# Seven block products in two more token groups of the shared experts, with the weight sums made in consecutive items

## The reference, cut to what matters

```python
for e in range(N_SHARED):                       # 2 shared experts
    h = silu(x_flat @ s_w1[e].T) * (x_flat @ s_w3[e].T)
    shared_out = shared_out + h @ s_w2[e].T
...
s = sigmoid(router_in @ W_router.T);  sel = s + router_bias   # top 2 of 8, gates from s
for e in range(N_EXPERTS):
    h = gelu(x_flat @ r_w1[e].T)
    routed_out = routed_out + h @ r_w2[e].T * gates_full[:, e:e + 1]
out = (shared_out / 2 + routed_out) / 4
```

## Time and profile before

| what | us |
|---|---|
| median of three runs | 1938.53 |
| the profiled execution, first to last instruction | 1936.9 |
| TensorE busy | 1899.1 (98%) |
| VectorE busy | 1166.6 (60%) |
| ScalarE busy | 898.0 (46%) |
| DMA engines, mean busy share | 48.3% on the SyncE queues' hardware queue, 10.0% on GpSimd's |

### The profile page before, as it was taken

One profiled execution on the slowest core, in us unless ns is written; L12 is line 12 of the kernel. 1 busy time (PEld: TensorE's weight loads), 2 busy tenths in 40 slices (PEclk: granted clock), 3 DMA queues, 4 the chain that ended last, 5 costly groups with the idle time before them and its releaser, 6 DMA issues. The chain is left out here.

```text
span 1936.9 us, 47260 instructions
## 1 busy us (share of the span) xinstructions
PE 1899.1 (98%) x18896; PEld 1230.9 (64%) x18896; DVE 1166.6 (60%) x2564; ACT 898.0 (46%) x1900; POOL 155.9 (8%) x160
## 2 busy tenths in 40 slices
PE   8999989999999999999999999999999999999997
PEld 7999954444444434444444444457777777899996
DVE  6666646554788656312111116778778886688887
ACT  4444445434112444434333335534334443588886
POOL 0000000000000000211111102111111120000000
PEclk8999999999999999999999999999999999999999
DMA  7033347866353565899999957655454566142233
GB/s 307 14 130 130 132 150 196 236 201 201 129 174 136 174 210 165 194 238 219 216 219 206 199 135 235 195 178 162 138 160 135 159 153 240 57 165 47 47 56 48
DMA packets 305823, 314.02 MB, mean 162 GB/s; under 512 B 228887, under 2 KB 246429, under 8 KB 298718
## 3 DMA queue, kind: packets, MB, share of 16 engines
q1 hardware_dynamic: 292526, 267.53, 48.3%
q0 software_dynamic: 13104, 43.79, 10.0%
HBM read 191.98 MB, written 73.66 MB: 137 GB/s over the span
## 5 line engine op out<-in xcount | busy, mean ns | idle before, releaser
L1275 PE MATMUL sh_p<-xh,arena 128*128 128x512 f16 x1280 | 382.1, 380 | 6.2 <-ACT sh_gated L1550 4.7
L1346 PE MATMUL p<-sh_h_hi,arena 128*128 128x512 f16 x1024 | 304.6, 379 | 1.0 <-DVE sh_h_lo L1925 1.0
L1275 PE MATMUL sh_p<-xl,arena 128*128 128x512 f16 x640 | 243.2, 380 | 0.0
L2286 DVE SCALAR_TENSOR_TENSOR ro_hs<-ro_h,fac,ro_hs 128x512 f16<-128x512 f32 x71 | 53.4, 751 | 297.2 <-ACT ro_hs L2272 297.2
L1275 PEld LDWEIGHTS sh_p<-xh,arena 128*128 128x128 f16 x1280 | 125.2, 98 | 158.8 <-ACT sh_gated L1550 5.2
L2229 PE MATMUL ro_py<-arena,ro_ht 128*128 x852 | 195.0, 379 | 1.8 <-DMA ro_ht<-ro_hs 1.8
L1346 PE MATMUL p<-sh_h_lo,arena 128*128 128x512 f16 x512 | 194.0, 379 | 0.0
L1521 ACT CAST sh_h_hi<-sh_gated 128x512 f16<-128x512 f32 x128 | 79.1, 618 | 231.8 <-DVE sh_gated L2018 205.5
L1346 PEld LDWEIGHTS p<-sh_h_hi,arena 128*128 128x128 f16 x1024 | 96.6, 98 | 107.1 <-DVE sh_h_lo L1925 2.2
L2229 PEld LDWEIGHTS ro_py<-arena,ro_ht 128*128 128x128 f16 x852 | 83.3, 98 | 102.5 <-issue 2.3
L1285 PE MATMUL sh_p<-xh,arena 128*128 128x256 f16 x672 | 118.0, 273 | 0.5 <-DVE sh_u L1904 0.4
(11 more groups left out here) (331 smaller groups left out, 3923.5 us busy)
## 6 DMA issues: line engine op xcount, KB each, us to landing
stage<-in_shared_w SPq DMA_DIRECT2D x29, 768.0 KB, 5.5
routed_rows<-xres SPq DMA_DIRECT2D x71, 256.0 KB, 3.1
stage<-in_norms_r SPq DMA_DIRECT2D x16, 1024.0 KB, 5.2
stage<-in_routed_w SPq DMA_DIRECT2D x16, 1024.0 KB, 6.1
stage<-in_norms SPq DMA_DIRECT2D x14, 1024.0 KB, 5.5
arena<-x SPq DMA_DIRECT2D x12, 1024.0 KB, 5.8
x<-xres SPq DMA_DIRECT2D x16, 512.0 KB, 2.6
x_rows<-arena SPq DMA_DIRECT2D x8, 1024.0 KB, 9.5
```

The costliest lines, as they stand in the source:

```text
L1275: mm = nc.tensor.matmul(p1[u % P1][:], arena[:, w:w + P], x[slot(gl)][:, :, k, :], start=(j == 0), stop=(j == 3 * KD - 1))
L1346: mm = nc.tensor.matmul(p2[m][:], arena[:, w:w + P], h[n % 2][:], start=(i == 0 and j == 0), stop=(i == HID - 1 and j == 2))
L2286: nc.vector.scalar_tensor_tensor(hs[t % TURNS][:, D:2 * D], h[t % 2], fac[:, 3:4], hs[t % TURNS][:, 0:D], ALU.mult, ALU.subtract).then_inc ...
```

## The change

In the first half, groups 2 and 3 (items 32 to 63) are made with seven block products. All 16 tiles are mixed in consecutive items, loads in items 8 to 23. The row sums start at item 15, the routing at item 30, its scales at item 36; all 16 routed matrices are split from item 48 on, at the end of ScalarE's item. Scratch places move: two of the routed matrices' places (12 and 14) hold token sums first, the rings of mixed weights and two of the partial sums lie in `mix` and `mixed` once the mixing is done, and a bank of PSUM gets other columns. `brow`, `b_lo` and `b2` share a tile with the raw token sums. The weight quarter s3 is loaded from `mixed` in DRAM in items 17 to 32.

```diff
-MIX_AT = tuple(range(14, 24, 2)) + tuple(range(40, 62, 2))
+MIX_AT = tuple(range(8, 24))
 X_BLOCKS = 7
-BLOCK_AT = (7, 8, 9, 11, 12, 13, 14)
-RAW_AT = (10, 10, 11, 12)
+PLAIN_GROUPS = (2, 1)
+X_ORDER = (("b11", "b21", "b22", "t1", "t2", "t4", "t3"), ("b11", "b21", "b22", "t1", "t3", "t2", "t4"))
+BLOCK_AT = ((8, 9, 10, 11, 12, 13, 14), (7, 8, 9, 11, 12, 13, 14))
+RAW_AT = ((10, 11, 12, 13), (10, 10, 11, 12))
+EXTRA_MATRIX = (12, 14)
+LATE_MATRICES = ((11, 48), (13, 49), (15, 50), (0, 51), (1, 52), (12, 53), (2, 54), (3, 55), (4, 56), (5, 58), (6, 59), (7, 60), (8, 62), (9, 63), (10, 64), (14, 64))
...
+    FULL = PLAIN_GROUPS[part]
+    S0 = FULL * HID
...
-        ROUTE_AT = look_at(LOOKS)
-        NORM_AT = ROUTE_AT + 1
-        SCALE_AT = NORM_AT + NORMS_R
-        order = [b for b in range(2 * EXPERTS) if matrix_end(b) is None] + [b for b in range(2 * EXPERTS) if matrix_end(b) is not None]
-        E_AT = SCALE_AT + 3
...
+        ROUTE_AT = look_at(LOOKS) + 4
+        NORM_AT = LOADED - AHEAD + 1
+        SCALE_AT = ROUTE_AT + 6
+        order = [b for b, _ in LATE_MATRICES]
+        split_at = lambda j: LATE_MATRICES[j][1]
...
-        plain = lambda n: first_part or n < HID
+        plain = lambda n: n < S0
...
                     if e >= 2:
                         sp.wait_ge(y_second, e - 1)
+                    elif first_part:
+                        sp.wait_ge(mix_stored, 16 * HID)
...
-                    sp.wait_ge(p1_filled, 2 * i + 2)
+                    sp.wait_ge(p1_filled, 2 * (S0 - HID + i) + 2)
+                    if first_part:
+                        sp.wait_ge(mix_stored, 16 * (hidden(i) + 1))
...
-                    if not first_part and n in (HID - 4, HID - 3):
-                        load_mixed(n + 4)
-                    if not first_part and HID <= n and n + 1 < ITEMS and n > HID:
+                    if S0 - n in ((3, 2) if first_part else (4, 3)):
+                        load_mixed(n + (3 if first_part else 4))
+                    if S0 < n and n + 1 < ITEMS:
                         load_mixed(n + 1)
-                    if not first_part and 1 <= n <= HID:
-                        load_s3(n - 1)
+                    if 0 <= n - 1 - (S0 - HID) < HID:
+                        load_s3(n - 1 - (S0 - HID))
...
                     if not plain(n):
                         second(n - 2)
                         last_three(n)
-                    elif n and (first_part or n < HID - 1):
+                    elif n and n < S0 - 1:
                         second(n - 1)
-                if not first_part:
-                    second(ITEMS - 2)
+                second(ITEMS - 2)
                 second(ITEMS - 1)
...
                     if not plain(n):
                         gate_left(n)
-                if not first_part:
-                    gate_right(ITEMS - 1)
-                    high_h(ITEMS - 1)
+                    if first_part:
+                        for j in range(2 * EXPERTS):
+                            if n == split_at(j):
+                                split_matrix(j)
+                gate_right(ITEMS - 1)
+                high_h(ITEMS - 1)
...
-                    pool.wait_ge(p1_filled, 2 * (PART_GROUPS - 1) * HID)
+                    pool.wait_ge(y_second, (PART_GROUPS - 1 - FULL) * HID)
```

More of the change, by code:

```diff
@@ L892, in shared_part @@
             mix, mixed = sb("mix", [P, MIXES * QUARTER]), sb("mixed", [P, MIXES, 2, QUARTER], F16)
+            flat = mixed[:].rearrange("p s h n -> p (s h n)")
+            ring_pair = [mix[:].bitcast(F16)[:, i * 4 * QUARTER:(i + 1) * 4 * QUARTER] for i in range(2)]
+            ring_one = [flat[:, i * 2 * QUARTER:(i + 1) * 2 * QUARTER] for i in range(2)]
+            v1, u2 = (flat[:, (4 + 2 * i) * QUARTER:(6 + 2 * i) * QUARTER].bitcast(F32) for i in range(2))
         else:
@@ L952, in shared_part @@
             assert at[0] <= EBASE + 4 * KD * CW + 2 * KD * GW + 2 * GROUP_TILES * D
+            extra = {}
+            for gl, matrix in zip(range(FULL, PART_GROUPS), EXTRA_MATRIX):
+                at[0] = RBASE + matrix * 2 * MATRIX
+                extra[gl] = scratch(3 * KD // 2 * CW, "p (b h k n) -> p b h k n", F16, b=3, h=2, k=KD // 2)
             mix_in, mix_sum, mix_hi, mix_lo, mix_stored = (sem(n) for n in ("mix_in", "mix_sum", "mix_hi", "mix_lo", "mix_stored"))
@@ L1198, in _ @@
                         load_x(1)
-                    if i == (1 if first_part else 2) and gl:
+                    if i == (1 if first_part and plain(n) else 2) and gl:
                         store_x(gl - 1)
@@ L1426, in _ @@
                         pe.wait_ge(list_ready, u + 1)
+                        if u == 0:
+                            pe.wait_ge(chain, ROUTED + 5)
                         for i in range(LISTED):
@@ L1495, in split_block @@
                     if b >= 3:
-                        act.wait_ge(t_raw, 4 * (gl - 1) + b - 2)
-                    if b == 4 and gl == 2:
+                        act.wait_ge(t_raw, 4 * (gl - FULL) + b - 2)
+                    if b == 4 and first_part:
+                        act.wait_ge(xt_stored, 16 * LOOKS)
+                        if gl == 3:
+                            act.wait_ge(chain, ROUTED)
+                    elif b == 4 and gl == 2:
                         act.wait_ge(lo_stored, 16)
@@ L1562, in _ @@
                         split_tile(n + AHEAD)
-                    if not first_part and i in BLOCK_AT and gl + 1 < PART_GROUPS:
-                        split_block(gl + 1, BLOCK_AT.index(i))
+                    if i in BLOCK_AT[part] and FULL <= gl + 1 < PART_GROUPS:
+                        split_block(gl + 1, BLOCK_AT[part].index(i))
                     if first_part and n - 1 in MIX_AT:
@@ L2035, in _ @@
                         add_rows(*returned(n - 1))
-                    if i == (0 if first_part else 1) and gl:
+                    if i == (0 if first_part and plain(n) else 1) and gl:
                         leave(gl - 1)
@@ L2041, in _ @@
                         mix_sums(MIX_AT.index(n - 1))
-                    if not first_part and gl + 1 < PART_GROUPS:
-                        for r in range(len(RAW_AT)):
-                            if i == RAW_AT[r]:
+                    if FULL <= gl + 1 < PART_GROUPS:
+                        for r in range(len(RAW_AT[part])):
+                            if i == RAW_AT[part][r]:
                                 raw_block(gl + 1, r)
-                        if i in BLOCK_AT:
-                            low_block(gl + 1, BLOCK_AT.index(i))
+                        if i in BLOCK_AT[part]:
+                            low_block(gl + 1, BLOCK_AT[part].index(i))
                     if first_part:
```

119 lines of the change are left out of this document (61 added, 58 removed).

## The result

The changed kernel takes **2114.59 us** (median of four runs, 2112.22 to 2117.28) against 1938.52, a ratio of 1.0906 (95% interval 1.089 to 1.0921). The forecast was 2084 with a range of 2018 to 2130: sign and size hold, 31 us too low. The profiled execution is the longest of the four; it spans 2115.6 us.

The account below looks back on a forecast made before the run. PE, busy 98%, was taken as the bound. Terms -19.2 - 4.7 + 146 + 9 + 2 + 8 + 2.8 + 1.5 = +145.4 on 1936.9 us gave 2082.3, as median 2084 us; range 2018 to 2130.

Parts of the forecast that it names:

- Part 1: Matmuls of the 32 seven-block items: 0.60 us less each, -19.2 us, and -4.7 for PE's one stall at late mixings.
- Part 2: Mixing loop, items 10 to 24: each turn waits for a store behind SyncE's queue; 269.6 us for 15 items, +146.
- The token store: Item 17: SyncE stores token group 0 and waits for it before loading group 2, ahead of the transposes; +10 us.
- The bounds (+91 to +189): Range of the mixing loop's +146: every store landing in 3 us below, every store taking 10.2 us above.
- Part 3: Seven-block items, 32 to 63: list parts +9, maximum +2, matrix splits +8, step, drain and first sum +2.8, last matrices +1.5.
- The list parts' +9: Items 38 to 45 carry list parts, 40 to 46 token sums: turns of 7.5 to 8.9 us, +9 (0 to 14).
- The matrix split's +8: In 14 of items 48 to 63 a split behind gate_left delays last_sums, PE late by 0.6 us each: +8 (0 to 25).
- The step and the maximum (2.8 + 2): Step into seven-block items, with drain and a first sum, +2.8 us; item 37's maximum on PE waiting for owners, +2.
- (a): Rival: in the mixing loop only VectorE's own chain binds, stores land in time; +30, with the seven-block terms 1968 us; chance 0.10.
- (b): Rival, faster: the mixing loop stays hidden, every turn ending within PE's 7.8 us; 1921 us; chance 0.05.
- (c): Rival, slower: VectorE's 8.9 us turn holds in all 32 seven-block items as small waits add; 2115 us; chance 0.04.
- (d): Rival: the items meant for seven blocks stay plain; 2099 us with the mixing loop; chance 0.01.

Follow-up runs that it names:

- experiment 1: The kernel before with only its mixing item numbers changed, to 8 to 23, all items plain: 2038.3 us.
- experiment 7: ScalarE's half of the matrix split moved ahead of gate_left: 2103.38 us on the changed kernel, 1996.68 on the changed kernel with spaced mixings.
- experiment 8: The changed kernel with the routing three items earlier, from item 27: 2107.87 us.
- experiment 5: The changed kernel with two raw-weight buffers, mixing load ahead of the store, store one item earlier, and matrix split ahead of gate_left: 2000.16 us.
- experiments 1 and 3: Experiment 1 has its own line; 3 is the changed kernel with the mixed tile's store issued one item earlier, ahead of the next mixing load: 2025.03 us.
- experiment 2: The changed kernel with all four groups of the first half plain again, mixing still in items 8 to 23: 2105.18 us.

## Why the prediction was right, and where it fell short

Against the profiled execution the forecast was 2082.3 us, and the span is 2115.6: 33 us. They lie in three places: 16 in the loop, 14.5 in items 25 to 63, 3 behind item 63.

**Bound and place: right.** PE had 98%, and everything else was hidden until an order, not an amount of work, broke it. The loss is where it was put, in items 10 to 24, by the mechanism named: SyncE released by the low part, the store behind the transposes, the cast behind the landing.

**Part 1: right in its unit.** The 42 matmuls of 128x256 of a seven-block item, here `last_three` and the next `first_four` in a row on PE (its timeline: the first row of the 42 and the first behind them):

```profile
691.54 0.38 PE L1303 MATMUL sh_p<-xh,arena 128*128 128x256 f16 x2
...
696.13 0.59 PE L1364 MATMUL p<-sh_h_hi,arena 128*128 128x512 f16 x2
```

696.13 - 691.54 = 4.59 us, as forecast, 109 ns each. The Trainium skill's figures (TensorE: Matmul & The Clock Gate, Back-to-back issue gap) would have made the 42 dearer than the 24 they replace; the trace shows no such thing. The late stall also went, and was worth more than its 4.7 us: where only the mixing was moved, items 47 to 63 take 6.4 us less than before (the first pair of matmuls behind the stall, too, took 1.03 us in place of 0.59). But the 0.6 us an item is worth something only where PE sets the turn: the casts are less than a plain item's 7.8 us apart in 8 of the 32.

**Part 2: right in its chain, the landings too short.** The gating product of item 10 was to start at 356.2 and did at 356.1. The turns of items 10 to 24 sum to 279.3 against 269.6. The term that was mis-sized is "I take 6 us behind transposes and such a load ... and 8 behind two large ones". The fifteen landings sum to 123 us, where this gives 110: those behind transposes and one load took 6.2 to 7.1, those in a look's third turn 6.4 to 9.1, and those in its first turn, behind the store of the turned rows and a load, 9.5 to 10.2. The token store took 3 us less than my 10, as turn 18 took 27.1 us against 20 for the other late second turns; the rest of the chain, issues and cast to end, holds within a microsecond in all turns but that of item 22 (1.5 longer). Set against experiment 1, the row sums cost these turns 56.5 us, 5.1 for each of the eleven that have their load ahead. That is 2.3 us on DVE, 0.5 of issue and 2.9 of landing in the mean (0 to 4.3). I had listed 20.1 for them, but the landing was inside the 6 and the 8. That PE gives 6 us back afterwards didn't hold: the cast of item 25 is the full 162 late, and items 25 to 31 return 2.6. The bounds (+91 to +189) hold it.

**Part 3: too small, and wrong by its own sign.** It was to be wrong if its items took over 8.5 us outside of the list parts; items 47 to 63 took 8.6 in the mean. The list parts' +9 was 6: items 38 to 47 take 70.9 us where 9 x 7.2 would be 65. The matrix split's +8 is the term that failed. I counted DVE's late start against PE's slack, once for each item ("PE is late by 0.6 each"), and didn't close the chain through `gate_left`'s wait for the low part. It is a ring of its own, so nothing is regained from item to item: items 47 to 63 take 137.6 us where 16 x 7.2 = 115 would be PE's, 22 more, of which experiment 7 gave 11 back by one edit. Of the other 11, PE's waits for the mixed weights are 6.6 us there. I had put the moved loads at nothing, because "after item 25 SP has no transposes left"; but it issues two in item 58, and the mixed weights' load stands behind them. A row had shown the price: the 1.4 us that I took from the earlier trace rows for the step is a wait for a load from `mixed`, at 1311 us, 27 us behind the step itself. The step and the maximum (2.8 + 2) were to leave items 31 to 38 near 55; they took 63.6, 8.5 over the plain kernel of experiment 1, and experiment 8 shows most of that to be routing steps on the step, which I had at nothing but for the maximum. Drain: PE waited once for the last low part, 4.0 us, for which I had 1.0 from the earlier trace rows.

**Rivals.** (a) is out: all 15 casts that had a store before them waited for it. Its 147 us for the fifteen turns were not reached even in experiment 5 (175.6). (b) is out with the first turn. (c), DVE's turn of 8.9 us in all 32 items, is partly true: 8.1 to 8.8 us did hold in 15 of them, by list parts and by the ring through ACT, not by small waits; that 2114.6 meets its 2115 is chance, as the loop was 16 us longer, too. (d) is out: L1303 runs from item 32.

## What to carry to other kernels

When steps that share a buffer move from every second item to every item, close the ring: follow one buffer from its release round to its next release, through the queue's order, with every DMA issue that stands in between and with what is in flight ahead of the one you wait for. If the ring is longer than an item, its length is the new turn, however idle all engines are; and the repair can be one instruction moved in one queue (90 us here). Also ask what a saved microsecond of the bounding engine needs from the others: seven block products save PE 0.6 us an item and give DVE two more (six operations of 0.42 to 0.75 us in place of two of 0.7), and in the first half that paid in no kernel run here. A load that is new beside such items needs the same care: look for what stands ahead of it in its queue, there too.

## What the runs showed of the hardware that I had not expected

- A 512 KB store landed in 2.8 to 3.4 us after its issue when nothing large was ahead on its queue (kernel before, experiments 1 and 3), in 5.9 to 8.6 behind one transfer of 768 or 1024 KB, in 7.7 to 10.2 behind two (experiment 1 and the changed kernel).
- In the loop the granted clock fell to 0.72 to 0.80 of 2.4 GHz while PE worked half of the time. It did not set these turns: between 356 and 636 us DVE waited 0.4 us for PE and ACT not at all. The clock was back at 1.00 in the stretch 636 to 683, right behind the loop.
- At the start of the routed experts PE's sequencer waited 1.3 to 1.4 us in all profiled executions but that of experiment 2, where it waited 8.7 (its row below). Both executions of that kernel took the same time within 0.3 us, so the wait may belong to the kernel and not to the execution; the runs don't show which. A difference of medians under some 7 us is better told apart by the casts' distances inside the stage, and those repeat within 2 us in most rows of the ruler, though items 33 to 38 took 42 in three kernels and 39.4 in others with nothing changed there.

```profile
PE ro_pf L2258 <- PEq L1075: 8.7, 1, 8.7
```
